# Two bias sums moved from GpSimd to TensorE, a copy of layer 3's input less one kept by ScalarE, and a new written-out order on every engine

## What is computed

```python
# layer 0 (stage A): pairwise scores, layernorm over all pairs, leaky relu, softmax, sigmoid(alpha @ x)
# layer 1 (stages B and C)
h = x @ Wp + bp; attn = softmax(mask(leaky(src + dst)));  h_gat = relu(layernorm((attn * adj) @ h) * g + b)
z = relu(layernorm(((1 + eps) * h_gat + adj @ h_gat) @ W1 + b1) * mg + mb)
x = layernorm(x + relu(z @ W2 + b2 + h_gat))
# layer 2 (stage D)
x = layernorm(x + (A * I) @ (x @ W[0]) + (A * (1 - I)) @ (x @ W[1]) + bias)
# layer 3 (stage E)
h = x @ W; attn = softmax(mask(leaky(src + dst)))
x = layernorm(x + elu(attn @ h))
```

## Time and profile before

| | |
|---|---|
| time, median of 3 runs | 1177.85 us (1176.78 to 1179.11) |
| the profiled execution: its own time, its span | 1178.55 us, 1176.8 us |
| busy PE / DVE / ACT / POOL | 92% / 85% / 81% / 54% of the span |
| granted TensorE clock, mean | 0.973 of full |

### The profile page before, as it was taken

How to read it: one execution, slowest core, us unless ns; L and a number is a source line. 1 busy time by engine, 2 the same in 40 slices (tenths; PEclk the granted TensorE clock), 3 DMA queues, 4 the chain that set the end, 5 groups by cost and what they waited for, 6 DMA issues and landing times. The chain is left out here.

```text
span 1176.8 us, 27392 instructions
## 1 busy us (share of the span) xinstructions
PE 1082.7 (92%) x7562; PEld 879.5 (75%) x7562; DVE 1004.7 (85%) x2807; ACT 953.5 (81%) x2421; POOL 639.6 (54%) x1282
## 2 busy tenths in 40 slices
PE   4688999999999999999999999999999989999863
PEld 2456688877877888877877888877877787778753
DVE  4887899999999999999999999999999889886742
ACT  1556789898888889888888889888888888888653
POOL 4124545666665555656665555656665545564432
PEclk8788999999999999999999999999999999999986
DMA  3000001101101110100101110100101100100000
GB/s 94 28 28 19 28 11 36 36 19 35 36 27 36 36 36 27 36 27 27 36 27 36 36 36 27 36 31 22 36 27 36 47 28 19 38 28 10 28 9 18
DMA packets 59473, 36.12 MB, mean 31 GB/s; under 512 B 3872, under 2 KB 54816, under 8 KB 59424
## 3 DMA queue, kind: packets, MB, share of 16 engines
q1 hardware_dynamic: 59424, 35.54, 9.7%
HBM read 18.75 MB, written 8.39 MB: 23 GB/s over the span
## 5 line engine op out<-in xcount | busy, mean ns | idle before, releaser
L1014 PE MATMUL ps<-hE,pTE 128*128 128x128 f32 x1024 | 127.1, 276 | 0.0
L942 PE MATMUL ps<-xsA,pA 128*128 128x128 f32 x1024 | 126.5, 277 | 0.2 <-ACT xsA L2308 0.2
L1014 PE MATMUL ps<-hB,pTB 128*128 128x128 f32 x1024 | 123.7, 277 | 1.2 <-DVE y_D L1806 0.7
L1075 PE MATMUL ps<-att_j,xD 128*128 128x512 f32 x256 | 122.8, 603 | 0.7 <-ACT xD L2254 0.7
L1031 PE MATMUL ps<-gin_j,hgat 128*128 128x512 f32 x256 | 121.4, 599 | 0.0
L1014 PEld LDWEIGHTS ps<-hE,pTE 128*128 128x128 f32 x1024 | 120.9, 193 | 0.5 <-issue 0.5
L942 PEld LDWEIGHTS ps<-xsA,pA 128*128 128x128 f32 x1024 | 120.8, 194 | 0.5 <-ACT xsA L2308 0.5
L1014 PEld LDWEIGHTS ps<-hB,pTB 128*128 128x128 f32 x1024 | 119.2, 193 | 2.2 <-DVE pTB L1670 1.1
L2360 ACT ACTIVATE pE<-wE,mnE 128x512 f32<-128x512 f32 x128 | 92.7, 724 | 26.8 <-DVE mnE L1657 26.1
L2297 ACT ACTIVATE pA<-vA,nmA,rirA 128x512 f32<-128x512 f32 x128 | 105.2, 844 | 6.5 <-DVE vA L1727 6.4
L511 POOL TENSOR_TENSOR lnnm_D<-lnst_D,consts 128x4 f32<-128x4 f32 x32 | 7.5, 234 | 183.9 <-DVE lnst_D L1624 183.9
(11 more groups left out here) (235 smaller groups left out, 3019.5 us busy)
## 6 DMA issues: line engine op xcount, KB each, us to landing
xA<-in_x_dram SPq DMA_DIRECT2D x32, 256.0 KB, 2.7
xrA<-in_x_dram SPq DMA_DIRECT2D x32, 256.0 KB, 2.7
xrB<-xB SPq DMA_DIRECT2D x32, 256.0 KB, 2.2
out_dram<-xout SPq DMA_DIRECT2D x32, 256.0 KB, 2.2
adj_i<-in_adj_dram SPq DMA_DIRECT2D x1, 1024.0 KB, 5.2
a<-in_L_gnn_a_dram SPq DMA_DIRECT2D x2, 64.0 KB, 5.6
w_sb<-in_L_gnn_W_dram SPq DMA_DIRECT2D x2, 64.0 KB, 4.6
l2w<-in_L_gnn_W_dram SPq DMA_DIRECT2D x2, 64.0 KB, 4.1
```

What stands on the lines that cost most here:

```text
L942: last = mm(at("aggA")[:, i * P:(i + 1) * P], pA[:, j, i * P:(i + 1) * P], xsA[:, j], start=(j == 0), stop=(j == NT - 1))
L1014: last = mm(at("agg" + n)[:, i * P:(i + 1) * P], att[n]["pT"][:, i, j], att[n]["h"][:, j, 0:P], start=(j == 0), stop=(j == NT - 1))
L1075: last = mm(at("axD"), xD[:, j], att2_j[:, j], start=(j == 0), stop=(j == NT - 1))
```

## The change

POOL's two bias steps go. b2 and layer 2's bias become rows of `brows` like b1 (so the set-up splits 514 columns into three parts, not 258), and a 512-column bf16 product puts each into PSUM ahead of the f32 products of `x2_C` and `out_D`. q_C and y_D add hgat and xD themselves. A new ScalarE step, `minus_E`, writes `xEm = xE - 1` (128x512), and y_E becomes a plain sum of y1E and xEm; norm_D now waits for minus_E's reading of xE instead of y_E's. Stage C's and D's inputs are freed by q_C and y_D. And the lists `fill`, `turn` and `drain` of all engines, and the table of banks, are others throughout.

```diff
-            def bias_C(g):
...
-                pool.tensor_tensor(hgb[:], hgat[:], bias_2, ALU.add).then_inc(s["hgb_ready"], 1)
-
-            def bias_D(g):
...
-                pool.tensor_tensor(xDb[:], xD[:], bias_l2, ALU.add).then_inc(s["xDb_ready"], 1)
-
...
-                features("x2", zT, w2_sb[:]).then_inc(s["x2C_in_psum"], 1)
+                features("x2", zT, w2_sb[:], bias_2).then_inc(s["x2C_in_psum"], 1)
...
+                mm(tiles(at("outD")), onesb[:], bias_l2, start=True, stop=False, skip_group_check=True)
                 for i in range(NT):
                     dst = at("outD")[:, i * P:(i + 1) * P]
-                    mm(dst, axT[:, i * P:(i + 1) * P], l2w1[:], start=True, stop=False, skip_group_check=True)
+                    mm(dst, axT[:, i * P:(i + 1) * P], l2w1[:], start=False, stop=False, skip_group_check=True)
...
-                dve.wait_ge(s["hgb_ready"], g.now)
-                v.tensor_tensor(qC[:], tiles(at("x2")), hgb[:], ALU.add).then_inc(s["qC_ready"], 1)
+                v.tensor_tensor(qC[:], tiles(at("x2")), hgat[:], ALU.add).then_inc(s["qC_ready"], 1)
...
-                dve.wait_ge(s["xDb_ready"], g.now)
...
-                v.tensor_tensor(ln["D"]["y"][:], tiles(at("outD")), xDb[:], ALU.add).then_inc(s["y_D"], 1)
+                v.tensor_tensor(ln["D"]["y"][:], tiles(at("outD")), xD[:], ALU.add).then_inc(s["y_D"], 1)
...
+                dve.wait_ge(s["xEm_ready"], g.now)
...
-                v.scalar_tensor_tensor(ln["E"]["y"][:], y1E[:], -1.0, xE[:], ALU.add, ALU.add).then_inc(s["y_E"], 1)
+                v.tensor_tensor(ln["E"]["y"][:], y1E[:], xEm[:], ALU.add).then_inc(s["y_E"], 1)
...
-                act.wait_ge(s["xDb_ready"], g.last)
+                act.wait_ge(s["y_D"], g.last)
...
+                act.wait_ge(s["xEm_ready"], g.last)
+                normalise(g, "D", lambda i: ln["D"]["y"][:, i], xE)
+
+            def minus_E(g):
...
                 act.wait_ge(s["y_E"], g.last)
...
+                a.activation(flat(xEm[:]), flat(xE[:]), ACT.Identity, scale=1.0, bias=consts[:, 3:4]).then_inc(s["xEm_ready"], 1)
...
-                act.wait_ge(s["hgb_ready"], g.last)
+                act.wait_ge(s["qC_ready"], g.last)
...
-                t.run(bias_D, 4)
...
-                t.run(bias_C, 3)
```

In `fill`, DVE now takes much of the set-up (among it `select_rows0`, `select_rows1`, the cut of the bias rows) between the steps of graph 0's stage A, where it took most of it after them:

```diff
-                t.graph(0, dots_A0, dots_A1)
-                t.once(mask_adj)
...
+                t.graph(0, dots_A0, dots_A1, mean_A, sumsq_A)
+                t.once(mask_adj, totals, row_ranges, clip_count0, clip_count1, edge_numbers, select_rows0)
+                t.graph(0, v_A0)
+                t.once(select_rows1)
+                t.graph(0, v_A1)
+                t.once(edge_ranks, copy_w, clip_count2, clip_count3)
```

More of the change, by code:

```diff
@@ L326, in resnorm_gnn @@
[L326 to L330, removed]
@@ L1294, in drain @@
                 t.graph(GRAPHS - 8, agg_E3)
-                t.graph(GRAPHS - 5, pT_B2, agg_B0, pT_B3, agg_B1, agg_B2, agg_B3)
+                t.graph(GRAPHS - 5, pT_B2, agg_B0, agg_B1, pT_B3, agg_B2, agg_B3)
                 t.graph(GRAPHS - 4, agg_A0)
@@ L1412, in drain @@
-                t.graph(GRAPHS - 4, agg_E3)
-                t.graph(GRAPHS - 1, pT_B1, pT_B2, agg_B0, agg_B1, pT_B3, agg_B2, agg_B3)
-                t.graph(GRAPHS - 3, transpose_xE, h012_E, h3_E)
-                t.graph(GRAPHS - 2, ax_D0)
+                t.graph(GRAPHS - 1, agg_B0, agg_B1, pT_B3)
+                t.graph(GRAPHS - 3, transpose_xE)
+                t.graph(GRAPHS - 1, agg_B2, agg_B3)
+                t.graph(GRAPHS - 3, h3_E, h012_E)
+                t.graph(GRAPHS - 2, ax_D0, transpose_xD)
@@ L1937, in fill @@
+                t.graph(3, y_A)
+                t.graph(2, offset_B)
+                t.graph(3, bn_A)
+                t.graph(4, sumsq_A)
+                t.graph(0, L_E0, M_E0, L_E1, L_E2, L_E3, M_E1)
+                t.graph(1, diag_D)
+                t.graph(0, M_E2)
+                t.graph(4, v_A0)
+                t.graph(0, M_E3)
+                t.graph(4, v_A1, v_A2, lrelu_A0, v_A3)
                 t.graph(2, bn_Z)
-                t.graph(4, lrelu_A0, lrelu_A1, lrelu_A2)
+                t.graph(5, dots_A0)
@@ L2102, in drain @@
-                t.graph(GRAPHS - 2, dots_A1, mean_A, sumsq_A)
-                t.graph(GRAPHS - 4, gain_B, offset_B)
-                t.graph(GRAPHS - 3, y_A, bn_A)
-                t.graph(GRAPHS - 6, L_E0, L_E1, M_E0, L_E2, L_E3, M_E1, M_E2)
-                t.graph(GRAPHS - 2, v_A0, v_A1, lrelu_A0)
-                t.graph(GRAPHS - 6, M_E3)
-                t.graph(GRAPHS - 4, bn_Z)
-                t.graph(GRAPHS - 2, v_A2, v_A3, lrelu_A1, max_A, lrelu_A2)
-                t.graph(GRAPHS - 5, diag_D)
@@ L2111, in drain @@
-                t.graph(GRAPHS - 2, offset_A, lrelu_A3)
-                t.graph(GRAPHS - 3, L_B0, L_B1)
+                t.graph(GRAPHS - 4, zz_B, bn_B, ve_B)
+                t.graph(GRAPHS - 7, y1_E)
+                t.graph(GRAPHS - 2, dots_A1, mean_A)
+                t.graph(GRAPHS - 7, y_E)
+                t.graph(GRAPHS - 4, gain_B, offset_B)
+                t.graph(GRAPHS - 7, bn_E)
+                t.graph(GRAPHS - 2, sumsq_A)
+                t.graph(GRAPHS - 3, y_A)
+                t.graph(GRAPHS - 6, L_E0, L_E1, M_E0)
@@ L2187, in drain @@
-                t.graph(GRAPHS - 1, bn_Z)
-                t.graph(GRAPHS - 2, y_D, bn_D)
-                t.graph(GRAPHS - 1, q_C)
+                t.graph(GRAPHS - 1, mult_B2)
+                t.graph(GRAPHS - 2, y_C, bn_C)
+                t.graph(GRAPHS - 1, mult_B3, zz_B, bn_B, ve_B, gain_B, offset_B)
+                t.graph(GRAPHS - 4, y1_E)
+                t.graph(GRAPHS - 3, L_E0)
+                t.graph(GRAPHS - 4, y_E)
+                t.graph(GRAPHS - 3, L_E1, M_E0, M_E1, L_E2, L_E3, M_E2, M_E3)
@@ L2450, in fill @@
                 t.graph(1, relu_B)
+                t.graph(0, copy_axD)
                 t.graph(3, copy_rowsA)
```

1376 lines of the change are left out of this document (684 added, 692 removed), and 6 rows, old and new, of the table IN_BANK.

## The result

| | before | after |
|---|---|---|
| time, median (same chip, 4 runs each) | 1177.43 us (1176.78 to 1179.11) | 1156.42 us (1156.2 to 1157.6) |
| ratio | | 0.9821, 95% interval 0.9804 to 0.9838 |
| span of the profiled execution | 1176.8 us | 1154.5 us |
| thA (tanh_A) of graph 5 starts | 205.92 | 212.79 |
| from it to thA of graph 25, 20 turns | 660.10, 33.005 a turn | 643.46, 32.173 a turn |

The changed kernel is faster by 1.8%; 1161 was forecast. The last three rows cut the span in three: the fill is 6.9 us longer, 20 turns of the loop are 16.6 shorter, the rest is 12.6 shorter; -22.3 in all.

A forecast was written before the change was run, and what follows sets the result against it. The prediction took the interplay of PE, DVE and ACT, within 2 us of each other, to set the 33.0 us turn. Loop -16.5, fill +1.5 and drain -2 gave -17, so about 1161 us, range 1149 to 1178.

The forecast's parts named there:

- forecast case: Whole kernel: a turn of 31.95 to 32.7 us and a time of 1151 to 1172 us, chance 0.53.
- In the loop PE is on the path, so I count all of it: The two bias products on PE in the loop: +0.44 us a turn, 14.1 us over 32 graphs, counted in full.
- As POOL time this is worth nothing: POOL loses two bias steps, 2.7 us a turn; with POOL busy 418.5 of 693.1 us, no gain was counted.
- The spA chain: Stage A, squares_A to spA: 4.61 us falls to 3.67 without two collisions, 4.2 with one; 0.1 of waiting left.
- With little to spare: varA behind four DVE instructions after mean_A: DVE is ready about when PE is; waiting 0.1 us, bounds 0 and 0.63.
- The waits ahead of the transposes of stage B: PE's waits for exp_B and mult_B: 0.58 us a turn should fall to 0.1 to 0.3 by the new order.
- The turn: One loop turn: 31.85 + 0.4 = 32.25 us, 0.75 less than 33.00; 22 turns give -16.5 us, bounds -25 and +9.7.
- Such margins don't all hold: PE's waits in the loop: margins of 0.15 to 0.3 us, so of 1.6 us of waits 0.4 is left.
- Fill: Set-up before the loop: graph 0's exponentials start some 3 to 6 us later; +1.5 us taken, bounds -3 and +6.
- The fill decides: Slower rival: graph 0 is 6 us late, the loop gains only 2 to 3; 1182 us, chance 0.06.
- Drain: After the loop: four turns save some 0.5 to 1 us each; -2 us taken, bounds -6 and +3.
- minus_E at nothing: ACT's new step between copy_axD and exp_E0, about 0.5 us from start to start: costed at nothing, otherwise 11 to 14 us.

The follow-up runs named there:

- e1: The changed kernel without its two bias products in x2_C and out_D, order unchanged: 1153.69 us, ratio 0.9793, a turn of 32.17 us.
- e11: The kernel before, in its own order, with the bias sums as TensorE products and without POOL's two bias steps: 1172.85 us, ratio 0.9955.
- e8: The changed kernel with the bias sums back on POOL (bias_D ahead of rstd_Z, bias_C behind it), no bias products: 1186.56 us, ratio 1.0060.
- e12: The changed kernel with the bias sums on POOL, bias_D behind square_A, and no bias products: 1192.77 us, ratio 1.0125.
- e9: The kernel before with only VectorE's order around sumsq_A changed as in the changed kernel: 1187.88 us, ratio 1.0067.
- e4: The changed kernel with only POOL's triangles in the fill put back ahead of centre_A of graph 0: 1152.01 us, ratio 0.9771.
- e6: The changed kernel with one exchange in VectorE's turn, bn_Z behind v_A3 instead of ahead of it: 1169.81 us, ratio 0.9908.

## Why the prediction was right, and where not

The time, 1156.4, lies in the forecast case's range, in part by luck: several terms behind it were wrong and made up for each other.

- **"In the loop PE is on the path, so I count all of it"**: wrong. The products' 0.44 us a turn (0.22 each, as measured: out_D's from 645.65 to 645.87) cost 0.00 in the new order (e1) and nothing that shows in the old one (e11). A busy share of 98% isn't a path; the ring passes PE from agg_B1 to z_C, and the products stand outside that.
- **"As POOL time this is worth nothing"**: wrong, and the largest miss. POOL's two steps would cost 1.3 to 1.5 us a turn in the new order (e8, e12), by place and collisions, at a POOL that is busy 45%.
- **The spA chain**: without the two collisions 3.67 was expected, with one left 4.2. It is 637.03 - 633.04 = 3.99, one collision, and the wait is gone. A third stretched step, power_A, had been overlooked; its 0.25 us is most of what 3.99 lies below 4.2. varA isn't late in the changed kernel (0.32 us behind squares_A, as before), but the same edit alone makes it late and the kernel before slower (e9). "With little to spare" was the weak step.
- **The waits ahead of the transposes of stage B**: gone, as was xE's. Two of the causes weren't needed: without POOL's bias steps, and with the products, most of both is gone in the old order as well (e11). xB's wait, 5.1 in e11 as before, went only with the new order.
- **The turn**: 32.25 forecast, 32.17 measured, so -16.5 against -0.83 x 22 = -18.3. "Such margins don't all hold" gave 0.4 us of waits; the waits found are 0.26 in the loads for mult_B1 and, by starts, some 0.2 ahead of L888's products and 0.1 ahead of z_C. Right in size; the sum's parts (+0.44 on PE, -1.2 of waits) don't add up like this on a ring, so that it came within 0.08 us is luck too. How the -0.83 divides among the new order's places isn't known.
- **Fill**: +1.5 was taken with +6 as the bound; it is +6.9. Of it 1.5 to 3.4 are POOL's triangles behind centre_A (e4), which I hadn't costed. The rest isn't split further. The prediction had named a loop that starts more than 4 us later as a sign of being wrong, and the condition of its rival "The fill decides"; that came true (z_C of graph 4 at 223.59, before 214.42), but the loop and the drain made up for it.
- **Drain**: -2 was taken, -6 the bound; the rest is 12.6 shorter, of which one loop turn is 0.8. Only the wait per turn was moved over from the loop; the last graphs' stages, where PE has gaps, were left out: of 42.9 us without work for PE 13.9 went. The two errors, +5.4 and -10, have opposite signs.
- **minus_E at nothing**: not tried alone. xEm takes 0.72 us, not 0.5 to 0.6. Without the copy this order can't run, by the lists: the next graph's norm_D stands ahead of relu_E and expm_E, for which y_E waits.

## What to carry to other kernels

Where several engines are each above 85% in a loop, find the ring: follow one turn back from a wait to itself. Work off the ring cost nothing here as long as it fitted into a wait, even on the busiest engine, and an exchange that takes 0.3 us out of one place is worth nothing until the rings under it are known. Changes of arithmetic and of order have to be priced together: apart they gave -0.18 and +0.43 to +0.68 us a turn here, together -0.83.

## What was unexpected in the hardware

VectorE's mask, an instruction with one SBUF source (f32 in, bf16 out), took 3.74 us for four beside GpSimd's memset, its select and the start of its next step, 1.43 without the first two; `no_i<-adj_i`, 128x2048, took 2.29 us beside them before and 1.23 in the changed kernel. So not only instructions with two SBUF inputs are held up. And a GpSimd step that starts a moment behind a VectorE instruction with two SBUF inputs, or just ahead of it, can last until that ends: 0.64 and 0.76 instead of 0.2 us, and then 1.39 instead of 1.01 for a longer step, three times in a row in e6.
